# Banded and full attention with a transposed second score pass, masked by an integer product on GpSimd

## The reference

```python
# first layer's attention: 64 softmaxes (16 heads x 4 members) of head size 16 per batch, over all 128 keys
qh, kh, vh = (interfere(qh), interfere(kh), interfere(vh))
scores = jnp.einsum('bhqdm,bhkdm->bhqkm', qh, kh) / math.sqrt(dk)
weights = jax.nn.softmax(scores, axis=3)
out = jnp.einsum('bhqkm,bhkdm->bhqdm', weights, vh)
return out @ Wo.T + bo
# second layer's attention: 8 heads of size 16 over T = 1024 positions, window of 16 keys, zero padding at the ends
dots = jnp.einsum('bhdt,bhdtw->bhtw', qh, k_win) * scale
attn = jax.nn.softmax(dots, axis=-1)
out = jnp.einsum('bhtw,bhdtw->bhdt', attn, v_win)
return _pointwise(Wo, bo, out)
# second layer's feed-forward: a product, masked by rows and columns that a softmax over 64 clusters selects
out = jnp.where(query_sel[:, None] & row_sel[None, :], dense, jnp.zeros((), dense.dtype))
```

## Time and profile before

| | |
|---|---|
| three runs | 2406.6, 2407.38 (median), 2408.14 us |
| the profiled execution | 2407.05 us, its span 2405.4 us |
| busy, share of the span | PE 91%, PEld 73%, DVE 58%, ACT 41%, POOL 7% |
| granted PE clock, mean | 0.956 of full speed |
| DMA | 426.59 MB, mean 177 GB/s |

### The profile page before, as it was taken

How to read it: one execution, slowest core, us unless ns; L and a number is a source line. 1 busy time by engine, 2 the same in 40 slices (tenths; PEclk the granted TensorE clock), 3 DMA queues, 4 the chain that set the end, 5 groups by cost and what they waited for, 6 DMA issues and landing times. The chain is left out here.

```text
span 2405.4 us, 49290 instructions
## 1 busy us (share of the span) xinstructions
PE 2182.1 (91%) x17638; PEld 1766.2 (73%) x17638; DVE 1394.1 (58%) x2604; ACT 975.4 (41%) x2850; POOL 174.0 (7%) x225
## 2 busy tenths in 40 slices
PE   5999699999979999979978999959999996775998
PEld 4999689989957777758854777737777774564887
DVE  4443322112159999923325777649999995784664
ACT  2222221111059999900002111129999995440000
POOL 0000000000021212100000000010000000330000
PEclk9999899999989999989988999979999998886999
DMA  3223533332356777533323878775655653751221
GB/s 126 106 105 123 172 135 132 140 148 113 131 229 260 273 276 267 197 140 131 131 96 128 304 291 314 277 303 183 241 195 195 238 186 96 247 175 58 87 86 58
DMA packets 163583, 426.59 MB, mean 177 GB/s; under 512 B 14192, under 2 KB 90736, under 8 KB 151216
## 3 DMA queue, kind: packets, MB, share of 16 engines
q1 hardware_dynamic: 161200, 417.16, 47.2%
q0 software_dynamic: 2304, 8.39, 1.1%
HBM read 257.73 MB, written 167.77 MB: 177 GB/s over the span
## 5 line engine op out<-in xcount | busy, mean ns | idle before, releaser
L953 ACT ACTIVATE a_probs<-a_s_bank,a_nmax 128x128 f32<-128x128 f32 (+3 forms) x2176 | 598.8, 422 | 36.0 <-DVE a_nmax L893 36.0
L893 DVE TENSOR_REDUCE a_nmax<-a_s_bank 128x8 f32<-128x1024 f32 (+1 forms) x240 | 293.5, 1223 | 47.5 <-PE a_s_bank L999 23.8
L1009 PE MATMUL a_t_bank<-ident_sb,a_probs 128*128 128x128 f32 (+3 forms) x2176 | 286.2, 275 | 1.1 <-ACT a_pt L961 0.8
L1009 PEld LDWEIGHTS a_t_bank<-ident_sb,a_probs 128*128 128x128 f32 (+3 forms) x2176 | 225.0, 142 | 21.0 <-ACT a_probs L953 1.1
L907 DVE COPY a_pt<-a_t_bank 128x512 f32<-128x512 f32 (+3 forms) x272 | 177.1, 651 | 4.3 <-PE a_t_bank L1009 4.3
L961 ACT ACTIVATE a_pt<-a_t_bank 128x512 f32<-128x512 f32 (+3 forms) x272 | 165.0, 606 | 29.0 <-PE a_t_bank L1009 27.4
L1024 PE MATMUL a_o_bank<-a_pt,a_vpad 128*32 128x128 f32 (+3 forms) x4352 | 168.8, 273 | 0.5 <-DVE a_osb L914 0.5
L373 PE MATMUL q_qb<-q_xt_hi,wq_hi 128*128 128x256 f32 x512 | 145.5, 284 | 3.0 <-DVE wq_lo L248 3.0
L373 PE MATMUL kv_kb<-kv_ct_hi,wk_hi 128*128 128x256 f32 x512 | 145.0, 283 | 3.0 <-DVE wv_lo L248 3.0
L373 PE MATMUL kv_kb<-kv_ct_lo,wk_hi 128*128 128x256 f32 x512 | 144.9, 283 | 0.0
L373 PE MATMUL kv_kb<-kv_ct_hi,wk_lo 128*128 128x256 f32 x512 | 144.9, 283 | 0.0
(11 more groups left out here) (200 smaller groups left out, 4563.6 us busy)
## 6 DMA issues: line engine op xcount, KB each, us to landing
a_qs<-q SPq DMA_DIRECT2D x32, 1024.0 KB, 6.1
a_ks<-k SPq DMA_DIRECT2D x32, 1024.0 KB, 8.1
k<-f_shared SPq DMA_DIRECT2D x64, 512.0 KB, 4.2
a_qs<-q SPq DMA_DIRECT2D x16, 2048.0 KB, 7.8
a_ks<-k SPq DMA_DIRECT2D x16, 2048.0 KB, 11.9
k<-kv_raw SPq DMA_DIRECT2D x32, 512.0 KB, 4.8
k<-kv_k_lo SPq DMA_DIRECT2D x32, 512.0 KB, 4.8
a_vraw<-v SPq DMA_DIRECT2D x32, 512.0 KB, 10.4
```

The source lines that it names most:

```text
L893: dve.tensor_reduce(nmax[0:m, k, :], scores(s)[0:m], X, ALU.max, negate=True).then_inc(maxed, 1)
L953: a = act.activation(probs[0:m, k, h, :], scores(s)[0:m, h, :], ACT.Exp, bias=nmax[0:m, k, h:h + 1])
L1009: a = pe.transpose(t_bank[:, h // 4, h % 4 * P:h % 4 * P + m], probs[0:m, k, h, :], e.ident[0:m, 0:m])
```

## The change

In both attention stages the exponentials are no longer transposed; the scores are computed a second time, transposed.

- The first pass is as before, but into one buffer of s_bank, and its only result is nmax. The maxima of a group of 4 units (layer 1: 3) are transposed in one PE instruction (`turn_max`) into n_bank, copied by ACT to nrow, and written by DMAs on ACT's queue (`shift`) into rows 0 and 64 of the q tile in SBUF. The k tile has ones there, which `setup` stores once into e.k0 and e.k1; the stores of k leave these rows alone, and the parts of q and k are reordered so that this row was the low part of q by the low part of k of one component.
- The second pass (`score_t`) multiplies k by q with operands exchanged, so that st_bank has keys on partitions and the maxima already subtracted. One activation per unit makes the exponentials of all 8 heads (pt, two buffers, in layer 1 three).
- In layer 1 this pass has no additive mask. GpSimd multiplies the bits of the exponentials, as 32-bit integers, by 1 or 0 (`mask`, bandi). The padding at the ends comes in as an extra term of the denominators (pad_in, pad_exp, pad_sel; at the edge tiles only).
- The values are products of vz with pt, two per 32 output rows, and eight further products with ones give each row's denominator. The output stays transposed: `divide` takes a reciprocal of 128 x 128 (layer 1: 128 x 112 or 120) and one product into att. Both transposes back and both copies go.
- att is stored transposed, in one DMA per batch. "wo" and `select` read it so and drop their transposes of it, and `select` its copy.
- Position tiles have 112 queries (120 at both ends). Scores run 9 units ahead of the division instead of 4; q and k have four slots for two.

```diff
-TSTEP = P - WIN + 1
+TSTEP = P - WIN
+K_ROWS = ((0, slice(1, 16)), (0, slice(17, 32)), (1, slice(0, 32)), (2, slice(0, 32)), (3, slice(0, 32)))
...
+            for k in (e.k0, e.k1):
+                sp.dma_start(k[:, 0:32:16, 0, :], unit[:]).then_inc(unit_out, 16)
...
+            def mask(u, s, i):
+                m = un.rows(s)
+                kind = {None: 1, 0: 0, 1: 2}[un.edge(s)]
+                pool.wait_ge(expd, done(u))
+                p = pt[:, s % D3, :, 0:m]
+                pool.tensor_tensor(p.bitcast(I32), p.bitcast(I32), bandi[:, kind, 0:m].unsqueeze(1).to_broadcast([P, UH, m]),
+                                   ALU.mult).then_inc(masked, 1)
...
+            def divide(u, s, i):
                 m, k = un.rows(s), s % 2
                 dve.wait_ge(valued, done(u))
...
+                dve.reciprocal(rinv[:, k, 0:m], o_bank[:, 0, P:P + m]).then_inc(inv, 1)
+                dve.wait_ge(inv, u + 1)
...
+                dve.tensor_tensor(att[:, slot, to], o_bank[:, 0, 0:m], rinv[:, k, 0:m],
                                   ALU.mult).then_inc(normed, 1)
-            staggered(dve, B * upb, un.per_loop, [(4, maximum), (2, turn_out), (1, value_out), (0, divide)])
+            staggered(dve, B * upb, un.per_loop, [(0, divide), (L - 1 + E, pads), (L + 1 + E, maximum)])
...
+                act.wait_ge(st_done, done(u))
+                act.wait_ge(valued, free(u, D3))
+                act.activation(pt[:, s % D3, :, 0:m], by_head(st_bank[:, 2 * k:2 * k + 2, :])[:, :, 0:m],
+                               ACT.Exp).then_inc(expd, 1)
+            def shift(u, s, i):
+                if not un.group_last(s):
+                    return
...
+                act.wait_ge(turned, g + 1)
+                act.wait_ge(shift_in[k], 16 * shifts * nth)
+                act.activation(nrow[:, k, 0:mg], n_bank[0:R, 0, 0:mg], ACT.Copy).then_inc(rowed, 1)
+                act.wait_ge(rowed, g + 1)
+                if layer == 0:
+                    act.dma_start(qs[0:65:64, s // 4, :, :].bitcast(F32), nrow[:, k, :].bitcast(F32)).then_inc(shift_in[k], 16)
+                    return
...
+            staggered(act, B * upb, un.per_loop, [(2 + E, exponential), (L - 2 + E, pads), (L + E, shift)])
...
-                pe.wait_ge(expd, free(u))
+                pe.wait_ge(maxed, free(u, 1))
...
+            def score_t(u, s, i):
+                slot, js, q, k = place(s)
+                m, st = un.rows(s), 2 * (s % 2)
+                if un.group_first(s):
+                    nth = un.groups // 2 * i + s // G // 2
+                    pe.wait_ge(shift_in[s // G % 2], 16 * shifts * (nth + 1))
+                pe.wait_ge(expd, free(u))
...
+                        a = pe.matmul(st_bank[:, st + half, j * P:j * P + m], ks[at, slot, js.start + j, k],
+                                      qs[at, slot, js.start + j, q], start=True, stop=True,
+                                      skip_group_check=True)
...
+                pe.wait_ge(masked if layer else expd, done(u))
+                pe.wait_ge(normed, free(u, 1))
...
-            staggered(pe, B * upb, un.per_loop, [(4, score), (2, turn), (1, value), (0, turn_back)])
+            staggered(pe, B * upb, un.per_loop, [(L + 1 + E, score), (2 + E, score_t), (1, value), (L + E, turn_max)])
```

504 lines of the change are left out of this document (260 added, 244 removed).

## The result

The changed kernel is slower. Its profiled execution takes 2538.27 us (span 2536.6) against 2407.05; the ratio to the kernel before is 1.052, 95% interval 1.0478 to 1.0562. Forecast were 2357 us and a range of 2325 to 2440, so the sign was wrong and the time outside the range.

What follows compares the result with a forecast made beforehand. PE was to bound the banded stage at 2.66 us a step, a ring over DVE the first at 2.38; -24 - 13 + 2 - 12 - 4 + 1 = -50 us took 2407 to 2357, range 2325 to 2440.

Steps and rivals of the forecast that it cites:

- PE in the banded stage waiting for nobody: Banded stage: expected trace sign that PE sets the pace without waits, 135 full steps of 2.66 us, stage -13 us.
- the ring: First stage: values, reciprocal, product, reduction, next scores close once per step, 2.38 us, longer than PE's 2.22.
- term k: DVE's reciprocal in both attention stages: growth of 4.1 ns an element, so 0.69 us at 128x128.
- Rival B: Attention stages: the reciprocal is slow and DVE's ring the bound; at 8.4 ns an element 2432 us; chance 0.12.
- filling and draining of the first stage: First stage's ends: 7 steps of 2.0 us, 2 mixed of 2.2, and 9 without scores of 1.6.
- rival D: Maxima reach the q tile too late: 2411 us at 5.5 us, slower at 8.3; chance 0.10.
- I charge DVE nothing: Banded stage: GpSimd's mask doesn't slow DVE, whose reduction took 1.22 us and copy 0.41 beside such an instruction.
- PE's banded step: Banded stage: PE's work for one unit falls from 2.82 us to 2.66 on the mean, up to 2.85.
- Filling and draining of the banded stage: Banded stage's ends: 6 steps of 2.5 us and 3 of 2.6 to fill, 9 of 2.4 to drain.
- rival C: Banded stage: integer product slower than float, GpSimd bounds; mask of 3.03 us gives +99, 2456 us; chance 0.16.
- the doubled value phase: PE in the first stage: eight more value products add 0.39 us to 0.57, or 0.57 at full cost.
- the output projection: After the first attention: eight PE transposes per tile go, 15 x 0.80 = -12 us.

Runs made afterwards that it cites:

- e_port: Changed kernel with a lead two units longer, PE's banded loop written out and DVE's padding addition reading PSUM: banded stage 438.2 us.
- h_port: First stage, its stores and output projection from the kernel before; banded stage and selection changed, with e_port's edits: ratio 1.0072, banded stage 432.0 us.
- e_dense: Changed kernel plus 256-column products in filling, draining and once a unit, both attention stages: first stage 592.9 us, banded 547.3.
- e_copy_dense: As e_dense, with the reciprocal replaced by a copy: first stage 580.3 us, banded 525.3.
- e_hold: Changed kernel, both PE loops written out, longer banded lead, 512-column products in the first stage's filling, draining and every unit: first stage 429.3 us, banded 451.1.
- e_hold0: As e_port, first-stage loop also written out, eight 512-column products after each of its first scores, none in its steady state: first stage 412.5 us.
- e_fill8: Changed kernel, longer lead and written-out loop in banded stage, eight 512-column products after each of the first stage's first scores: first stage 453.2 us.
- e_copy: Changed kernel with the reciprocal replaced by a copy of the same shape in both attention stages: first stage 492.9 us, banded 502.6.

## Why the prediction was wrong

The first stage was to lose 24 us and gained 24, the banded one was to lose 13 and gained 121. All else was right within 2 us. In the banded stage the step that failed is "PE in the banded stage waiting for nobody": the forecast is 135 steps of 2.66 us without a term for the maxima's transfer, the jumps, DVE's slower additions or the clock. In the first stage it is the ring, in its size and in its way, and again the clock.

- **The reciprocal** (term k = 4.1 ns, 0.69 us): measured 6.3 ns and 0.957 us. I had taken off an ordinary instruction's growth from the raw 5.6 ns, where the raw number was nearer. Against 2.38 the step of 2.57 is 119 x 0.19 = 23 us of the 48 that the first stage missed. Rival B names the reciprocal, at a price (8.4 ns) that wasn't met.
- **The ring.** The prediction closes it over the reduction and the next scores; PE never waits for nmax in the steady part, and the ring that holds the step goes from the product to the next values, over the one buffer of o_bank. That it was to be 2.38 us and is 2.57 looks like a mere error of size, but this is luck: with 6.3 ns the predicted ring gives 2.65, and the two rings happen to be nearly of one length (the maximum ends 0.06 us before the next scores start). Where they differ, the prediction was far off: in the draining, 9 steps of 1.6 us against 2.57 at full clock, 9 us.
- **The clock in filling and draining of the first stage.** Both were priced at full clock, and no step of the prediction had the clock in it. Up to 725 a lone score with its maximum took 2.44 us (forecast 2.0) and a full step 3.76; from 1025 on the draining steps took 3.42 instead of 2.57. By these rows that is some 14 us (an estimate), which with the 9 above makes up nearly all of the other 25.
- **The maxima's transfer** (rival D, 0.10): it failed where I called it mild, on the rule that queues take turns by packets. It came 8 to 13 us after its issue. Only eleven of 48 groups were late, 26.6 us in all. The longer lead was worth 71, but with it went waits for the addition below, and the half clock behind both; the runs don't separate these.
- **The jump of the loop** was not in the prediction at all, though the diff says 36 units a body and twice the value products: 19 us of gaps, 23 with what follows.
- **"I charge DVE nothing"** for the mask rested on a reduction and a copy that read PSUM. The change's own addition and its minimum read SBUF. Cost: 1.7 us a batch, 27 us over 16, at full clock; moving one operand gave 13 back. The minimum still reads SBUF in e_port and takes 0.39 us on the mean there, against 0.23 beside the short mask.
- **PE's banded step** (2.66 on the mean): right without that disturbance, 2.65; with it 2.83, so the 23 us (144 x 0.16) that this term should have gained were never there.
- **Filling and draining of the banded stage**: raising the clock there gave 11 us (432.0 to 420.6, of which I can't tell how much is filling).
- Right: the mask's own time (rival C out: 2.09 us, and 1.7 us of waits for it), the doubled value phase (1.04 us against 0.96), PE's undisturbed step, the output projection, the selection, the start and the stores.

The known pieces of the banded stage's 121 us, in the order in which they were taken away: 84 for lead and loop together, 13 for the addition, then 24 are left, of which 6 lie between e_port and h_port, unexplained, 11 were the clock at the ends, and 6 remain. What stays open: why the changed first stage's clock comes back after 17 us in one case and not for 430 in another, while in the banded stage it was back within 17 us in the changed kernel and took 34 to 38 in e_dense and e_copy_dense. Added whole-array products went with a clock that held in e_hold, but in e_dense and e_copy_dense, with fewer and shorter ones, not; e_hold also had no jumps, and I can't tell from these runs which of this counts. Nor is it known what the gaps in written-out code (e_hold0) are, or why the jumps of e_fill8 have gaps.

## What to carry over

Sum a change at both levels of the clock: a new wait of PE, or a longer filling, can be paid a second time by what runs slow behind it. Follow every buffer that has only one slot, and close each ring by itself: here the one that was overlooked set the step. A small transfer that a step depends on can be as late as the burst of loads that it is issued into, so place it by issue order and not by bytes; and mind the length of a loop's body on the busiest engine before doubling it. When work goes to GpSimd, price DVE's instructions with two SBUF operands by a row of such instructions, not by those that read PSUM.

## What was not expected of the hardware

- PE busy for 430 us at 1.2 GHz without the clock rising (e_copy), and 2.4 GHz held for 280 us with PE busy 85% of them.
- A gap of 5.1 to 5.3 us at a jump back in a body of 36 units in the old kernel, none at 18; and the same body of 16 units with gaps of 3.3 us and more at its jumps in e_fill8, without any in the changed kernel.
- Three transfers of 3.5 KB that PE gets 12.9 us after their issue, beside 4 MB on another queue.
- A DVE addition of 260 ns taking 995 on the mean, and up to 2.1 us, beside a GpSimd instruction of 2.1 us; a 128x128 reciprocal 957 ns against 292 for a copy.
